# Gated network's first blocks: unpacking of down rows one block apart, earlier first rows, third unpacking pass of the last pieces on ScalarE

## The chip, the cores and the metric

The kernel runs on one core of a Trainium2 chip. The metric is device microseconds from start to end of one launch; 1810.05 is the median of three runs of the kernel before (1808.7 to 1810.61). The engines are TensorE (PE: matmuls), VectorE (DVE), ScalarE (ACT), GpSimd (POOL) and SyncE (SP: issues transfers). Each works through its own instruction list in order and waits only on semaphores.

## The reference, cut to what matters

Four layers run one after the other on x (8 x 256 rows of 512); this case lies in the first two.

```python
x = x + gamma * softmax_attention(layernorm(x), ctx, ctx)   # channels attend, 8 heads of 64
w_gu, w_down = fp4 codes * group scales                     # 4-bit values, packed 8 to a word
gate, up = layernorm(x) @ w_gu.T                            # 2 x 1408 columns
y = (silu(gate) * up) @ w_down.T
x = x + y / sqrt(mean(y * y) + eps)
x = x + quantised_attention(...)                            # not touched
x = x + ternary_ffn(...)                                    # not touched
```

## The kernel before, in words

**Mixing stage** (`mix_rows`, about 0 to 350 us). Sixteen tiles of 128 rows. In step j (j from -3 to 15, one per tile) TensorE makes the transposed scores of tile j (`tscore`, psT) and the row-major scores of tile j+1 (`score`, psS, three banks), weighs with `weigh` (psO, psE) behind slots 6 and 11 and at the end, and turns the row maxima (`turn_maxima`). A step has 16 slots n = 0 to 15, and on each engine the tables at the head of the function say in which slot a piece of work is issued. VectorE's main work is `greatest`: 16 row maxima of psS per tile, one bank each. A score into a bank waits until the maximum of the bank's former score is taken. Then `split` cuts the maxima into three parts, which TensorE turns, and `maxima_rows` makes of them what the next tile's scores subtract. ScalarE does the exponentials (`exp`), GpSimd the subtractions that make queries and keys (`queries`, `keys`), the first Newton steps (`roots`) and the end of a tile (`finish`).

**The packed weights.** The 512 x 2816 gate and up weights come as four row groups, each cut into four pieces of 704 columns: 16 pieces, k = 0 to 15. `unpack(k, i)` on VectorE takes a piece through three passes over 128 x 704: i = 0 shifts each word (`move_bits`), i = 1 masks it (`keep_bits`), i = 2 multiplies by 2^126 into f16 (w_gu). Piece k belongs to step k + 3; `BITS` names the slots of its three passes. Pieces 11 and 12 belong to step 14, pieces 13, 14 and 15 to step 15; of a step's pieces all but the first follow at the step's end, three passes each.

**First rows.** At the start of step 15 VectorE normalises the first 512 rows (`first_rows`). ScalarE rounds them to f16 in four quarters (`first_high`, slots `FIRST`), GpSimd makes the four remainders (first_lo), and two transposing transfers bring both to first_xT. The first gate product waits for both.

**Gated stage** (`gated_ffn`, about 350 to 700 us). Four columns t of 512 rows, in each 11 blocks p; m = 11 t + p counts them. A block is, on TensorE, 8 gate matmuls, half of the down matmuls that are due (`down`, from block m - 3), 8 up matmuls and the other half. Of the four row groups ScalarE scales two (`scale`, g_psG to g_sum), VectorE the other two (`fold`), GpSimd adds them (totalled). A block's groups go through four banks, so the up matmuls of a block wait for the gate's `scale` and `fold`. ScalarE's silu and VectorE's product (`hidden`, g_hT) of block m - 1 follow in block m. In the first column each block also unpacks a 128 x 512 piece of the down weights: `unpack_down` (VectorE, two passes, L799 and L804), `value_down` (ScalarE, L1025), `scale_down` (GpSimd, L876), all three for piece p in block p, so that ScalarE waits in block p for VectorE's passes of the same block before it comes to the scales of block p + 1. In blocks 5 to 8 follows a quarter of the next column: `normalise` (VectorE, L895), `high_part` (ScalarE, L998), `low_part` (GpSimd, L869).

Of the kernel before, what the change touches and what calls it, by code (L numbers as in the profile page):

```python
# [6 lines left out]
F32 = mybir.dt.float32  # L7
# [12 lines left out]
NT = TOK // P  # L20
# [20 lines left out]
SUBNORMAL = 2.0 ** -24  # L41
LOW_BYTES = 0x00FF00FF
LOG_SET = "natural_log_exp_and_others"


Programs = namedtuple("Programs", "sync gpsimd vector scalar tensor")
# [211 lines left out]
def mix_rows(env, x_in, ctx_in, ctxT_in, gu_in, gus_in):  # L258
# [13 lines left out]
    NT3 = 3  # L272
    NG = NU + 1
    WEIGH = (6, 11)
    FIRST = (10, 11, 12, 13)
    CUT_K, NORMAL, CUT_Q = (3, 5), (7, 8, 11, 12), (9, NU - 1)
    INVERT, STATS = (5, 8, 11, 14), (2, 13)
    UNPACK = {j: (j - 3,) for j in range(3, NT - 2)}
    UNPACK.update({NT - 2: (11, 12), NT - 1: (13, 14, 15)})
    BITS = (6, 10, 13)  # L280
    SCORES = [1 + (n in (1, 4, 7, 10)) if n < 12 else 0 for n in range(NU)]
    FIRST_SCORE = [sum(SCORES[:n]) for n in range(NU)]
    FETCH_GU = (2, 3, 8, 11)
# [2 lines left out]
    with ExitStack() as ctx:  # L286
# [6 lines left out]
        def sem(name):  # L293
# [47 lines left out]
        inverted, mixed_s, added, after_s, bits_s = (  # L341
            sem(f"m_{n}") for n in ("inverted", "mixed", "added", "after", "bits"))
        gu_loaded = [sem(f"m_gu_loaded{g}") for g in range(CH)]
        first_xn, first_hi, first_lo, scales_in = (
            sem(f"m_{n}") for n in ("first_xn", "first_hi", "first_lo", "scales_in"))
        xn, halves = xs[(NT - 3) % 3], (qs[(NT - 3) % 3], ks[(NT - 3) % 3])

        def rows4(src, j):
# [12 lines left out]
        def invert(v, j, h):  # L361

            if h == 0:
                v.wait_ge(o_read, 2 * (j + 1))
                if j:
                    v.wait_ge(mixed_s, j)
            at = slice(h * P, (h + 1) * P)
            v.reciprocal(rinv[:, at], e_sums[j % 2][:, at]).then_inc(inverted, 1)  # L368

        def after(v, j):  # L370

# [148 lines left out]
        def scalar(act):  # L520
            def roots(j):

                act.wait_ge(varied, HT * (j + 1))
                if j:
                    act.wait_ge(guessed, j)
                act.activation(lnv[:, :], mv[j % 2][:, :, 1], ACT.Ln, bias=eps[:, :]).then_inc(lnv_ready, 1)
                act.wait_ge(lnv_ready, j + 1)
                if j >= 2:
                    act.wait_ge(normed, j - 1)
                act.activation(guess[j % 2][:, :], lnv[:, :], ACT.Exp, scale=-0.5).then_inc(guessed, 1)  # L530

            def cut_keys(j, k):

                half = slice(2 * k, 2 * k + 2)
                if k == 0:
                    act.wait_ge(c_in_s[j % 2], 64 * (j // 2 + 1))
                if j:
                    act.wait_ge(k_ready, HT * (j - 1) + 2 * k + 2)
                act.activation(k_sub[:, half, :], cs[j % 2][:, half, :], ACT.Copy,
                               scale=k_lo[:, :]).then_inc(k_cut, 1)  # L540

            def normalise(j, h):

                if h == 0:
                    act.wait_ge(normed, j + 1)
                act.activation(xs[j % 3][:, h, :], xs[j % 3][:, h, :], ACT.Identity, scale=ys[j % 2][:, h:h + 1],
                               bias=away[j % 2][:, h:h + 1]).then_inc(normal, 1)

            def cut_queries(j, k):

                half = slice(2 * k, 2 * k + 2)
                act.wait_ge(normal, HT * j + 2 * k + 2)
                if j:
                    act.wait_ge(q_ready, HT * (j - 1) + 2 * k + 2)
                act.activation(q_sub[:, half, :], xs[j % 3][:, half, :], ACT.Copy,  # L555
                               scale=q_lo[:, :]).then_inc(q_cut, 1)

            def exp(j, n):
                g = NU * j + n
                act.wait_ge(tscored, g + 1)  # L560
                if g >= RING:
                    act.wait_ge(pv_done, g - RING + 1)
                act.activation(prob[:, g % RING, :], psT[g % NT3][:, :], ACT.Exp,  # L563
                               scale=float(D0) ** -0.5).then_inc(exped, 1)

            def collect(j):

                b = j % 2
                act.wait_ge(pv_done, NU * (j + 1))
                if j >= 2:  # L570
                    act.wait_ge(mixed_s, j - 1)
                    act.wait_ge(added, j - 1)
                act.activation(weighed[b][:, :], psO[:, :], ACT.Copy, scale=gamma[:, :]).then_inc(o_read, 1)
                act.activation(e_sums[b][:, :], psE[:, :], ACT.Copy).then_inc(o_read, 1)

            def first_high(k):

                if k == 0:
                    act.wait_ge(tscored, NU * (NT - 2))
                act.wait_ge(first_xn, k + 1)  # L580
                act.activation(halves[0][:, k, :], xn[:, k, :], ACT.Copy).then_inc(first_hi, 1)

            def steps(j):
                for n in range(NU):
                    if has(j):
                        exp(j, n)
                    if n == 0 and has(j - 1):
                        collect(j - 1)
                    if has(j + 2):
                        if n == 2:  # L590
                            roots(j + 2)
                        if n in CUT_K:
                            cut_keys(j + 2, CUT_K.index(n))
                        if n in NORMAL:
                            normalise(j + 2, NORMAL.index(n))
                        if n in CUT_Q:
                            cut_queries(j + 2, CUT_Q.index(n))
                    if j == NT - 1 and n in FIRST:
                        first_high(FIRST.index(n))
            nc.scalar.preload_act_table_set(LOG_SET)  # L600
            act.wait_ge(masks, 14)
            turns(steps)
            collect(NT - 1)

        def vector(v):
            def statistics(j, h):
# [45 lines left out]

            def unpack(k, i):

                g, at = k // PER, slice(k % PER * UW, (k % PER + 1) * UW)
                words = raw_gu[:, g % 2, at]
                if i == 0:
                    v.wait_ge(gu_loaded[g], 16)
                    move_bits(v, env, words).then_inc(bits_s, 1)
                if i == 1:  # L660
                    v.wait_ge(bits_s, 3 * k + 1)
                    keep_bits(v, words).then_inc(bits_s, 1)
                if i == 2:
                    v.wait_ge(bits_s, 3 * k + 2)
                    v.tensor_scalar(env["w_gu"][:, g, at], words.bitcast(F32), 2.0 ** 126, None,
                                    ALU.mult).then_inc(bits_s, 1)

            def first_rows():

# [137 lines left out]
def gated_ffn(env, dn_in, dns_in, last_tile):  # L807

    nc, x_sb, mv, rstd = (env[n] for n in ("nc", "x_sb", "mv", "rstd"))
    with ExitStack() as ctx:  # L810
# [53 lines left out]
        def gpsimd(pool):  # L864
# [13 lines left out]
            for t in range(NTC):  # L878
                for p in range(FG):
                    m = FG * t + p  # L880
                    for i in SIDES:
                        a, b = part_sum[0][i][m % 3], part_sum[1][i][m % 3]
                        pool.wait_ge(folded, 4 * m + 2 * i + 2)
                        pool.tensor_tensor(a[:, :], a[:, :], b[:, :], ALU.add).then_inc(totalled, 1)  # L884
                    if t == 0:
                        scale_down(p)
                    if p in SPLIT and t + 1 < NTC:
                        low_part(t + 1, SPLIT.index(p))

        def vector(v):  # L890
# [60 lines left out]
            for t in range(NTC):  # L951
                for p in range(FG):
# [10 lines left out]
                            take_y(t - 1, 2 * i + 1)  # L963
                    if m:
                        hidden(m - 1)
                    if t == 0:
                        unpack_down(p)
                        if p == 3:
                            aggregate(v, env, 0, NT)
                        if p == 4:  # L970
                            invert_roots(v, env, 0, NT)
# [20 lines left out]
        def scalar(act):  # L992
# [30 lines left out]
            def value_down(f):  # L1023
                act.wait_ge(dn_bits, 2 * f + 2)
                act.activation(w_dn[:, f, :], w_dn[:, f, :], ACT.Copy, scale=2.0 ** 126).then_inc(dn_valued, 1)  # L1025

            for t in range(NTC):
                for p in range(FG):
                    m = FG * t + p
                    if m >= 3:  # L1030
                        act.wait_ge(h_ready, m - 2)
                    for i in SIDES:
                        scale(m, i)
                        if t and p == TAKE:
                            square_y(t - 1, 2 * i)
                            square_y(t - 1, 2 * i + 1)
                    if m:
                        silu(m - 1)
                    if t == 0:
                        value_down(p)  # L1040
                    if p in SPLIT and t + 1 < NTC:
                        high_part(t + 1, SPLIT.index(p))
            silu(FG * NTC - 1)
# [3 lines left out]
        def tensor(pe):  # L1047
# [7 lines left out]

            def gate_up(t, p, i):
                at = (i * FG + p) * P
                for g in range(CH):
                    q = CH * (2 * (FG * t + p) + i) + g
                    free(q - CH)  # L1060
# [1064 lines left out]
```

## Time and profile before

| | |
|---|---|
| median of 3 runs | 1810.05 us |
| the profiled execution | 1810.41 us, span 1808.6 us |
| TensorE busy | 1703.9 us (94%) |
| VectorE busy | 1499.0 us (83%) |
| ScalarE busy | 1256.8 us (69%) |
| GpSimd busy | 907.0 us (50%) |
| 60 to 350 us (mixing) | TensorE 271.12, VectorE 278.37, ScalarE 232.53, GpSimd 185.43 busy of 290; granted clock 1.00 |
| 350 to 460 us (gated, first column) | TensorE 98.62, VectorE 79.13, ScalarE 53.64, GpSimd 59.31 busy of 110; granted clock 0.93 |
| 460 to 700 us | TensorE 239.06, VectorE 172.47 busy of 240; granted clock 1.00 |

The span is what the profiler saw between the first and the last instruction; about 1.8 us lie around it. A timeline row gives start, duration, engine, line, operation, output and inputs, shape and count; in brackets stands how long the engine was idle before it and who released it. Rows of one kind that follow each other are merged. A chain row is a piece of the path that ended last.

### The profile page before, as it was taken

Reading aid. Unit: us, or ns where it says so; the run is one execution under the profiler, and the core shown is the slowest. Engines: PE = TensorE matmul, PEld = TensorE weight load, DVE = VectorE, ACT = ScalarE, POOL = GpSimd, SP = SyncE. Lnnn points to the kernel's source line nnn. Section 1 sums busy time; section 2 is a strip of 40 time slices with the busy share of each in tenths; the row PEclk is TensorE's granted clock in tenths of the full one; section 3 lists DMA queues with packets and bytes.
Section 4 is the critical chain, followed back from the end, with each engine's and each line's share of the span. In section 5 each row is a group of like instructions: output and inputs, shape, how many; then the busy total and the mean of one; then the engine's idle time right before and its main releaser. Section 6 shows DMA issues by size and latency. Waiting matters only on the chain.

```text
span 1808.6 us, 30394 instructions
## 1 busy us (share of the span) xinstructions
PE 1703.9 (94%) x10706; PEld 744.6 (41%) x10706; DVE 1499.0 (83%) x2796; ACT 1256.8 (69%) x2111; POOL 907.0 (50%) x927
## 2 busy tenths in 40 slices
PE   4999999889999999989999999999999998999999
PEld 1332323234444444434444444444444444444444
DVE  6899999877767669787999999999999998883332
ACT  5888888455554442333799999999999996774433
POOL 6567666256445430000488888888888884000000
PEclk9999999989999999999999999999999999999999
DMA  9866651301011005556666666666666567112020
GB/s 222 222 149 134 156 137 42 117 3 24 1 24 44 20 1 168 100 105 124 115 111 107 107 110 105 114 112 113 117 112 109 105 110 240 24 24 47 24 47 24
DMA packets 420631, 170.45 MB, mean 94 GB/s; under 512 B 382080, under 2 KB 391296, under 8 KB 419328
## 3 DMA queue, kind: packets, MB, share of 16 engines
q1 hardware_dynamic: 420480, 168.51, 45.5%
q8 instruction: 85, 1.39, 0.3%
q14 instruction: 66, 0.54, 0.1%
HBM read 69.89 MB, written 4.19 MB: 41 GB/s over the span
## 4 chain that ended last, share of the span: by engine, by line
PE 67%; DVE 19%; ACT 5%; issue 5%; POOL 2%; DMA 1%; SPq 0%; DVEq 0%; ACTq 0%; POOLq 0%
PE a_psM L1541 12%; PE a_psS L1589 9%; PE g_psY L1075 7%; PE g_psG L1062 7%; PE t_psD L2052 6%; DVE rmax L627 5%; PE t_psU L2039 5%; PE a_psO L1601 4%; PE k_psA L1459 3%; PE psO L762 3%; PE psE L765 2%; DVE maxima L1555 2%; ACT a_prob L1677 2%; POOL a_wide L1657 2%; DVE rinv L368 1%
## 5 line engine op out<-in xcount | busy, mean ns | idle before, releaser
L1555 DVE TENSOR_REDUCE maxima<-a_psM 128x1 f32<-128x512 f32 x1024 | 623.4, 681 | 1.9 <-PE a_psM L1541 0.2
L1677 ACT ACTIVATE a_prob<-a_psS,maxima,q_scale 128x1024 uint8<-128x1024 f32 x512 | 610.8, 1210 | 17.0 <-PE a_psS L1589 14.7
L1657 POOL CAST a_wide<-a_pairs 128x2048 int16<-128x2048 uint8 x256 | 484.0, 1900 | 98.0 <-DMA a_pairs<-a_prob 89.9
L1541 PE MATMUL a_psM<-KT,QO 128*128 128x512 bf16 x1024 | 367.5, 383 | 5.2 <-DVE k_kn L1382 1.6
L1589 PE MATMUL a_psS<-KT,QO 128*128 128x512 bf16 x1024 | 305.7, 380 | 3.1 <-ACT a_prob L1677 3.1
L1601 PEld LDWEIGHTS a_psO<-V,a_wide 128*128 128x128 f16 x4096 | 175.2, 96 | 140.5 <-DVE QO L1630 23.0
L1601 PE MATMUL a_psO<-V,a_wide 128*128 128x32 bf16 x4096 | 181.3, 177 | 16.4 <-DVE QO L1630 15.6
L905 DVE SCALAR_TENSOR_TENSOR g_sum<-g_psG,gu_scale,g_sum 128x512 f32<-128x512 f32 x176 | 124.1, 745 | 86.4 <-PE g_psG L1062 71.2
L884 POOL TENSOR_TENSOR g_sum<-g_sum 128x512 f32<-128x512 f32 x88 | 125.8, 1430 | 128.7 <-DVE g_sum L905 128.7
L563 ACT ACTIVATE prob<-psT 128x512 f32<-128x512 f32 x256 | 143.1, 599 | 60.7 <-PE psT L750 60.2
L1010 ACT ACTIVATE g_sum<-g_psG,gu_scale 128x512 f32<-128x512 f32 x176 | 111.5, 682 | 103.8 <-PE g_psG L1062 102.9
L627 DVE TENSOR_REDUCE rmax<-psS 128x1 f32<-128x512 f32 x256 | 158.6, 675 | 11.9 <-PE psS L736 9.7
L1075 PE MATMUL g_psY<-raw_dn,g_hT 128*128 128x512 f32 x352 | 163.1, 592 | 0.0
L1541 PEld LDWEIGHTS a_psM<-KT,QO 128*128 128x128 bf16 x1024 | 97.1, 96 | 132.2 <-DVE maxima L1555 127.2
L1864 DVE TENSOR_TENSOR t_hT_lo<-t_h,t_hT_hi 128x512 f16<-128x512 f32 x64 | 44.3, 692 | 123.4 <-ACT t_hT_hi L1991 123.3
L736 PE MATMUL psS<-ks,qs 128*128 128x512 f16 x256 | 91.1, 388 | 36.0 <-POOL qs L488 20.7
L1589 PEld LDWEIGHTS a_psS<-KT,QO 128*128 128x128 bf16 x1024 | 97.5, 98 | 66.7 <-ACT a_prob L1677 8.6
L1644 POOL TENSOR_TENSOR maxima<-maxima,q_scale 128x2 f32<-128x2 f32 x128 | 25.2, 197 | 190.0 <-DVE maxima L1549 190.0
L488 POOL TENSOR_TENSOR qs<-xs,q_sub 128x512 f16<-128x512 f32 x64 | 76.0, 1209 | 79.5 <-ACT q_sub L555 78.9
L1980 ACT ACTIVATE t_h<-t_psU,t_b 128x512 f32<-128x512 f32 x64 | 43.7, 682 | 92.6 <-PE t_psU L2039 92.6
L1677 ACT ACTIVATION_READ_ACCUMULATOR a_prob<-a_psS,maxima,q_scale 128x1 f32 x512 | 103.9, 203 | 0.0
L2052 PE MATMUL t_psD<-QO,t_hT_hi 128*128 128x512 f16 x256 | 97.1, 379 | 4.6 <-DVE x_sb L1875 3.4
(219 smaller groups left out, 2755.1 us busy)
## 6 DMA issues: line engine op xcount, KB each, us to landing
xs<-in_x SPq DMA_DIRECT2D x64, 256.0 KB, 6.9
cs<-in_ctx SPq DMA_DIRECT2D x64, 256.0 KB, 8.9
KT<-in_w SPq DMA_DIRECT2D x2, 4096.0 KB, 19.1
raw_gu<-in_gu SPq DMA_DIRECT2D x4, 1408.0 KB, 8.6
vs<-in_ctxT SPq DMA_DIRECT2D x16, 256.0 KB, 3.0
a_pairs<-a_prob SPq DMA_TRANSPOSE x256, 3.0
out<-x_sb SPq DMA_DIRECT2D x16, 256.0 KB, 2.6
x_sb<-in_x SPq DMA_DIRECT2D x1, 3584.0 KB, 14.4
```

Source lines behind the costliest of these rows:

```text
L563: act.activation(prob[:, g % RING, :], psT[g % NT3][:, :], ACT.Exp, scale=float(D0) ** -0.5).then_inc(exped, 1)
L627: v.reduce_max(rmax[j % 2][:, n:n + 1], psS[(NG * j + n) % 3][:, :], AX.X).then_inc(maxed, 1)
L884: pool.tensor_tensor(a[:, :], a[:, :], b[:, :], ALU.add).then_inc(totalled, 1)
L1062: mm = pe.matmul(psG[q % CH][:, :], w_gu[:, g, at:at + P], xT[t % 2][s][:, :, g, :], start=(s == 0), stop=(s == 1))
L1075: mm = pe.matmul(psY[k][:, :], hT[t % 2][:, f, k * P:(k + 1) * P], w_dn[:, f, :], start=(f == 0), stop=(f == FG - 1))
L1541: pe.matmul(psM[n % NM][:, :], QOf[:, i * P:(i + 1) * P], KTf[:, keys:keys + 512], start=True, stop=True).then_inc(shown, 1)
L1555: v.reduce_max(tops[i // JOIN % NB][:, i % JOIN, c:c + 1], psM[n % NM][:, :], AX.X).then_inc(topped, 1)
L1589: mm = pe.matmul(psS[g % NS][:, c * 512:(c + 1) * 512], QOf[:, i * P:(i + 1) * P], KTf[:, keys + c * 512:keys + (c + 1) * 512], start=True ...
L1601: mm = pe.matmul(psO[:, h * D1:(h + 1) * D1], wide[i % NV][:, parity, c, :].bitcast(F16), V[:, 2 * c + parity, h, :], start=(parity == 0 a ...
L1657: pool.tensor_copy(wide[i % NV][:, :, :, :].rearrange("p k c q -> p k (c q)"), both).then_inc(widened, 1)
L1677: act.activation(prob[i % NP][:, k * HK:(k + 1) * HK], psS[g % NS][:, :], ACT.Exp, scale=q_scale[:, i:i + 1], bias=bias[i // JOIN % NB][:, ...
L2052: mm = pe.matmul(psD[k][:, :], hT[s][:, g % RING, k * P:(k + 1) * P], w2q(f), start=(f == 0 and s == 0), stop=(f == FC - 1 and s == 1))
```

## The change

The diff has four parts.

1. `BITS` goes from (6, 10, 13) to (2, 6, 10). It holds for every step that unpacks, 3 to 15. `UNPACK` moves piece 12 from step 14's end to step 15.
2. `FIRST` goes from slots 10 to 13 to slots 7 to 10.
3. The third pass of pieces 12 to 15 moves from VectorE to ScalarE (`value_gu`): piece 12 in slot 12 of step 15, the others behind the last `collect`. The first gate product and the first up product wait for it. ScalarE loads the silu table ahead of the gated stage.
4. In the gated stage VectorE unpacks down piece m - 1 in block m (1 to 11), and ScalarE and GpSimd take piece m - 2 in block m (2 to 12).

```diff
-    FIRST = (10, 11, 12, 13)
+    FIRST = (7, 8, 9, 10)
+    LAST_GU = 12
...
-    UNPACK.update({NT - 2: (11, 12), NT - 1: (13, 14, 15)})
-    BITS = (6, 10, 13)
+    UNPACK.update({NT - 2: (11,), NT - 1: (12, 13, 14, 15)})
+    BITS = (2, 6, 10)
...
+            def value_gu(k):
+
+                act.wait_ge(bits_s, bits_of(k) + 2)
+                act.activation(gu_place(k), gu_words(k).bitcast(F32), ACT.Copy, scale=2.0 ** 126).then_inc(gu_valued, 1)
...
+                    if j == NT - 1 and n == 12:
+                        value_gu(LAST_GU)
...
             collect(NT - 1)
+            for k in range(LAST_GU + 1, CH * PER):
+                value_gu(k)
...
-                if i == 2:
+                if i == 2 and k < LAST_GU:
```

In the gated stage, on GpSimd, VectorE, ScalarE and TensorE in this order:

```diff
-                    if t == 0:
-                        scale_down(p)
+                    if 2 <= m < FG + 2:
+                        scale_down(m - 2)
...
+                    if 1 <= m <= FG:
+                        unpack_down(m - 1)
                     if t == 0:
-                        unpack_down(p)
...
+            nc.scalar.preload_act_table_set(SILU_SET)
...
-                    if t == 0:
-                        value_down(p)
+                    if 2 <= m < FG + 2:
+                        value_down(m - 2)
...
+                if t == 0 and p == 0:
+                    pe.wait_ge(env["gu_valued"], 1 + 3 * i)
```

VectorE's order in a mixing step, from the first maxima of a tile on (rmax: `greatest`; raw_gu with shift: first pass; raw_gu: second; w_gu: third). Before:

```order
L627 TENSOR_REDUCE rmax<-psS 128x1 x4
L613 BN_STATS stats<-xs 128x6
L627 TENSOR_REDUCE rmax<-psS 128x1 x4
L368 RECIPROCAL rinv<-e_sums 128x128
L627 TENSOR_REDUCE rmax<-psS 128x1
L799 TENSOR_SCALAR raw_gu<-raw_gu,shift 128x704
L627 TENSOR_REDUCE rmax<-psS 128x1 x3
L368 RECIPROCAL rinv<-e_sums 128x128
L627 TENSOR_REDUCE rmax<-psS 128x1 x3
L804 TENSOR_SCALAR raw_gu<-raw_gu 128x704
L627 TENSOR_REDUCE rmax<-psS 128x1
```

and after the change:

```order
L651 TENSOR_REDUCE rmax<-psS 128x1 x4
L637 BN_STATS stats<-xs 128x6
L821 TENSOR_SCALAR raw_gu<-raw_gu,shift 128x704
L651 TENSOR_REDUCE rmax<-psS 128x1 x4
L371 RECIPROCAL rinv<-e_sums 128x128
L651 TENSOR_REDUCE rmax<-psS 128x1
L826 TENSOR_SCALAR raw_gu<-raw_gu 128x704
L651 TENSOR_REDUCE rmax<-psS 128x1 x3
L371 RECIPROCAL rinv<-e_sums 128x128
L651 TENSOR_REDUCE rmax<-psS 128x1 x3
L688 TENSOR_SCALAR w_gu<-raw_gu 128x704
L651 TENSOR_REDUCE rmax<-psS 128x1
```

The first pass now stands ahead of the fifth maximum instead of behind the ninth, the second where the first stood, the third where the second stood; the place of the third, behind the split of the maxima, is empty.

ScalarE's order from the last exponentials of the mixing stage into the first gated blocks (qs<-xs: `first_high`; w_gu: `value_gu`; raw_dn: `value_down`). Before:

```order
L563 ACTIVATE prob<-psT 128x512 x2
L573 ACTIVATE weighed<-psO,gamma 128x512
L574 ACTIVATE e_sums<-psE 128x512
L1010 ACTIVATE g_sum<-g_psG,gu_scale 128x512 x4
L1025 ACTIVATE raw_dn<-raw_dn 128x512
L1010 ACTIVATE g_sum<-g_psG,gu_scale 128x512 x4
L1003 ACT_TABLE_LOAD
L1003 ACTIVATE g_sum<-g_sum 128x512
L1025 ACTIVATE raw_dn<-raw_dn 128x512
L1010 ACTIVATE g_sum<-g_psG,gu_scale 128x512 x4
```

and after the change:

```order
L601 ACTIVATE w_gu<-raw_gu 128x704
L578 ACTIVATE prob<-psT 128x512 x3
L588 ACTIVATE weighed<-psO,gamma 128x512
L589 ACTIVATE e_sums<-psE 128x512
L601 ACTIVATE w_gu<-raw_gu 128x704 x3
L1050 ACT_TABLE_LOAD
L1033 ACTIVATE g_sum<-g_psG,gu_scale 128x512 x8
L1026 ACTIVATE g_sum<-g_sum 128x512
L1033 ACTIVATE g_sum<-g_psG,gu_scale 128x512 x4
L1026 ACTIVATE g_sum<-g_sum 128x512
L1048 ACTIVATE raw_dn<-raw_dn 128x512
L1033 ACTIVATE g_sum<-g_psG,gu_scale 128x512 x4
```

The two exponentials at the head of the first excerpt are the last ones of the tile. In the second, ScalarE takes the piece of slot 12 and the three behind the tile's end, then loads the table; the scales of blocks 0 and 1 then follow each other with nothing of the down weights between them.

## Rows read from the trace of the kernel before

**Rows 1.** Chain of waits, 198 to 240 us: start, us, what (excerpt)
```profile
216.75 0.60 DVE rmax L627
...
217.48 0.38 PE psS L736
```

**Rows 2.** Timeline, VectorE, one tile: start, us, line, operation, count, [idle<-releaser]
```profile
213.66 2.48 DVE L627 TENSOR_REDUCE rmax<-psS 128x1 f32<-128x512 f32 x4
...
220.45 0.57 DVE L799 TENSOR_SCALAR raw_gu<-raw_gu,shift 128x704 int32<-128x704 int32 x1
221.15 1.89 DVE L627 TENSOR_REDUCE rmax<-psS 128x1 f32<-128x512 f32 x3
...
225.55 1.08 DVE L804 TENSOR_SCALAR raw_gu<-raw_gu 128x704 int32<-128x704 int32 x1
...
228.59 0.18 DVE L641 TENSOR_TENSOR rparts<-rrest,rparts 128x16 bf16<-128x16 f32 x1
...
229.28 0.51 DVE L665 TENSOR_SCALAR w_gu<-raw_gu 128x704 f16<-128x704 f32 x1
...
233.49 2.48 DVE L627 TENSOR_REDUCE rmax<-psS 128x1 f32<-128x512 f32 x4
```

**Rows 3.** Timeline, VectorE, tiles with no packed pieces
```profile
75.11 2.48 DVE L627 TENSOR_REDUCE rmax<-psS 128x1 f32<-128x512 f32 x4 [1.62 <-PE psS L736]
...
82.60 1.89 DVE L627 TENSOR_REDUCE rmax<-psS 128x1 f32<-128x512 f32 x3 [0.62 <-PE psS L736]
...
94.70 2.48 DVE L627 TENSOR_REDUCE rmax<-psS 128x1 f32<-128x512 f32 x4 [0.96 <-PE psS L736]
```

**Rows 4.** Timeline, TensorE, the tile of Rows 2
```profile
228.82 0.24 PE L774 MATMUL psS<-id_b,rparts 128*51 128x128 bf16 x1 [0.17 <-DVE rparts L641]
```

**Rows 5.** Timeline, GpSimd, the tile of Rows 2
```profile
218.30 4.85 POOL L477 TENSOR_TENSOR ks<-cs,k_sub 128x512 f16<-128x512 f32 x4
225.09 2.56 POOL L488 TENSOR_TENSOR qs<-xs,q_sub 128x512 f16<-128x512 f32 x2 [1.94 <-ACT q_sub L555]
```

**Rows 6.** Timeline, ScalarE, last tile and first gated blocks
```profile
337.26 2.06 ACT L563 ACTIVATE prob<-psT 128x512 f32<-128x512 f32 x4 [1.62 <-PE psT L750]
339.19 0.65 ACT L581 ACTIVATE qs<-xs 128x512 f16<-128x512 f32 x1
...
365.24 1.28 ACT L1003 ACT_TABLE_LOAD   x1
```

**Rows 7.** Timeline, GpSimd, last tile and first gated blocks
```profile
339.98 5.51 POOL L515 TENSOR_TENSOR ks<-xs,qs 128x512 f16<-128x512 f32 x4 [9.46 <-ACT qs L581]
...
362.40 2.49 POOL L884 TENSOR_TENSOR g_sum<-g_sum 128x512 f32<-128x512 f32 x2
```

**Rows 8.** Timeline, TensorE, first gate product
```profile
350.61 0.59 PE L1062 MATMUL g_psG<-first_xT_hi,w_gu 128*128 128x512 f16 x1 [4.09 <-DMA first_xT_lo<-ks]
```

**Rows 9.** Waits, 330 to 430 us: who waited for whom, us, times, longest
```profile
ACT raw_dn L1025 <- DVE raw_dn L804: 31.8, 9, 4.9
...
PE g_psG L1062 <- ACT g_sum L1010: 10.0, 6, 4.0
```

**Rows 10.** Timeline, VectorE, gated blocks
```profile
371.14 1.41 DVE L905 SCALAR_TENSOR_TENSOR g_sum<-g_psG,gu_scale,g_sum 128x512 f32<-128x512 f32 x2 [1.27 <-ACT g_sum L1010]
...
407.08 0.68 DVE L915 TENSOR_TENSOR g_hT<-g_sum 128x512 f32<-128x512 f32 x1
407.68 1.49 DVE L799 TENSOR_SCALAR raw_dn<-raw_dn,shift 128x512 int32<-128x512 int32 x1
409.21 0.43 DVE L804 TENSOR_SCALAR raw_dn<-raw_dn 128x512 int32<-128x512 int32 x1
...
414.50 0.68 DVE L915 TENSOR_TENSOR g_hT<-g_sum 128x512 f32<-128x512 f32 x1
```

**Rows 11.** Timeline, GpSimd, gated blocks
```profile
407.25 1.65 POOL L884 TENSOR_TENSOR g_sum<-g_sum 128x512 f32<-128x512 f32 x1 [0.47 <-DVE g_sum L905]
410.38 1.16 POOL L876 TENSOR_TENSOR raw_dn<-raw_dn,dn_scale 128x512 f32<-128x512 f32 x1 [1.49 <-ACT raw_dn L1025]
```

More of the change, by code:

```diff
@@ L43 @@
 LOG_SET = "natural_log_exp_and_others"
+SILU_SET = "silu_and_others"
 Programs = namedtuple("Programs", "sync gpsimd vector scalar tensor")
@@ L343, in mix_rows @@
         gu_loaded = [sem(f"m_gu_loaded{g}") for g in range(CH)]
-        first_xn, first_hi, first_lo, scales_in = (
-            sem(f"m_{n}") for n in ("first_xn", "first_hi", "first_lo", "scales_in"))
+        first_xn, first_hi, first_lo, scales_in, gu_valued = (
+            sem(f"m_{n}") for n in ("first_xn", "first_hi", "first_lo", "scales_in", "gu_valued"))
+        env["gu_valued"] = gu_valued
         xn, halves = xs[(NT - 3) % 3], (qs[(NT - 3) % 3], ks[(NT - 3) % 3])
@@ L368, in invert, with gu_words, gu_place, bits_of @@
             v.reciprocal(rinv[:, at], e_sums[j % 2][:, at]).then_inc(inverted, 1)
+        def gu_words(k):
+            return raw_gu[:, k // PER % 2, k % PER * UW:(k % PER + 1) * UW]
+        def gu_place(k):
+            return env["w_gu"][:, k // PER, k % PER * UW:(k % PER + 1) * UW]
+        def bits_of(k):
+            return 3 * min(k, LAST_GU) + 2 * max(0, k - LAST_GU)
         def after(v, j):
@@ L653, in unpack @@
             def unpack(k, i):
-                g, at = k // PER, slice(k % PER * UW, (k % PER + 1) * UW)
-                words = raw_gu[:, g % 2, at]
+                words = gu_words(k)
                 if i == 0:
-                    v.wait_ge(gu_loaded[g], 16)
+                    v.wait_ge(gu_loaded[k // PER], 16)
                     move_bits(v, env, words).then_inc(bits_s, 1)
                 if i == 1:
-                    v.wait_ge(bits_s, 3 * k + 1)
+                    v.wait_ge(bits_s, bits_of(k) + 1)
                     keep_bits(v, words).then_inc(bits_s, 1)
-                if i == 2:
-                    v.wait_ge(bits_s, 3 * k + 2)
-                    v.tensor_scalar(env["w_gu"][:, g, at], words.bitcast(F32), 2.0 ** 126, None,
-                                    ALU.mult).then_inc(bits_s, 1)
+                if i == 2 and k < LAST_GU:
+                    v.wait_ge(bits_s, bits_of(k) + 2)
+                    v.tensor_scalar(gu_place(k), words.bitcast(F32), 2.0 ** 126, None, ALU.mult).then_inc(bits_s, 1)
             def first_rows():
```

## The prediction

> **What bounds the kernel now.** I read the chain of waits first, then each engine's timeline around its stations. In the mixing stage the path changes between VectorE and TensorE. In a tile in the middle, the fifth row maximum ends a stretch of VectorE and releases TensorE's score [rows 1]: TensorE's score stands at 217.48, right behind the maximum's end at 217.35. The path then lies on TensorE (scores, weighing), and comes back to VectorE at 221.15, where the tenth maximum waits for a score: the first unpacking pass ended at 220.45 + 0.57 = 221.02, so it lay in time in which VectorE would have waited anyway [rows 2]. In a tile without packed pieces that gap is visible, 0.62 us idle at 82.60 [rows 3]. The last maxima, with the second pass between them, are on VectorE's path, and TensorE waits 0.17 us at the turn of the maxima [rows 4]. The third pass stands behind that, where TensorE weighs and nobody waits. So three passes (0.57 + 1.08 + 0.51 us [rows 2]) cost only 0.24 us of a tile: it takes 233.49 - 213.66 = 19.83 us [rows 2] against 94.70 - 75.11 = 19.59 without them [rows 3]. Their places decide.
>
> In the gated stage's first column ScalarE waits 31.8 us for VectorE's passes over the down words, and TensorE 10.0 us for ScalarE's scales behind them [rows 9]. That wait goes with the change. The question is who is late next.
>
> **How long a pass takes.** The pass of 1.08 us starts at 225.55, while a GpSimd instruction pair runs from 225.09 [rows 5]; a single one of that pair ends about 1.14 later (half of the pair, less what VectorE holds), at 226.23, and the pass ends at 226.63, 0.4 behind that [rows 2]. The pass at 220.45 meets the change from the second to the third of four GpSimd instructions that began at 218.30 [rows 5], near 220.58, and pays 0.57. The one at 229.28 meets none and pays 0.51. I take it that a pass costs 0.43 from start to the next start, plus the rest of the GpSimd instruction that it meets. The Trainium skill says so too (SBUF — State Buffer, Who interferes with whom): VectorE's two-port modes and GpSimd share a port pair, and the one that starts later is blocked for the other's whole instruction, while a tensor_reduce never is. The durations above agree. By that rule passes that meet GpSimd's work can't be counted at their own length, which speaks against two parts of this change.
>
> **BITS earlier, steps 3 to 12 (ten tiles).** The first pass now stands ahead of the fifth maximum, on the path. It meets only GpSimd's short steps there: 0.43 to 0.6, I take 0.5. TensorE's score and weighing are later by that. The second pass follows where the first stood, at 220.45 + 0.5 = 220.95, in the third of the four instructions, which (with the first pass gone from there) ends at 218.30 + 3 x 1.14 = 221.72. So it ends at about 222.15, where the tenth maximum stood at 221.15: it is now 1.0 later, of which TensorE's lateness hides 0.5. The third pass replaces the second. Queries' first instruction is 0.5 later too (225.6, ends 226.74), so the third pass, ready at 225.55 + 1.0, ends near 227.2 where the second ended at 226.63: VectorE is 0.6 late at the turn. TensorE, 1.0 late since the waited score, used to wait 0.17 there and is 0.83 late. The later of the two counts: 0.84 a tile, 8.4 us for ten. The empty place behind the split gives nothing back: TensorE weighs there. Bounds: if the second pass meets no instruction, 0.43 - 0.17 = 0.26 a tile, 2.6 us; if each pass meets a whole further one, 1.3 a tile, 13 us. In steps 13 and 14 there are fewer statistics ahead of the fifth maximum, and in 14 no queries and keys: from the same terms 0.6 + 0.2 = 0.8 us (0 to 1.5). Together 9.2 us later.
>
> **Piece 12 and FIRST.** VectorE has the first rows some 2.8 us sooner, but ScalarE's first quarter stands right behind an exponential that TensorE paces: at 339.19, behind four from 337.26 [rows 6]. Three exponentials of 0.48 now come behind it: 1.4 us. GpSimd's four remainders (339.98, 5.51 us [rows 7]) still alternate with VectorE's passes, now of pieces 13 to 15, so they start and end 1.4 sooner, and with them the first gate product at 350.61, which waits for the second transfer [rows 8]. It gains 1.4 us.
>
> **Third pass on ScalarE.** A 512-wide activation there takes 0.5 from start to start [rows 6], so 704 columns take about 0.7. One in slot 12 lies in waits for TensorE. Three behind the tile's end, 2.1 us, fall into the transfer's time, and so does a part of the table load, 1.28 us, which today stands ahead of the first silu [rows 6]. What sticks out delays the first fold, by my estimate by 0.4 us of those 1.28. The Trainium skill (ScalarE: Activation LUTs, What ACT_TABLE_LOAD costs) adds a drain of 1.38 us to each load; in this trace the next activation starts at once behind the load, and with the drain the sum below would be 1.4 us higher.
>
> **Down words one block apart.** TensorE and ScalarE no longer wait for the passes, so blocks 0 and 1 run into each other. Next late is GpSimd. It ends the last tile's `finish` behind VectorE's reciprocals, and then adds (two at 362.40, 2.49 us [rows 7]). With the net 1.4 - 0.4 = 1.0 us from above it starts them at 361.4 and ends at 363.9. The product of block 0 meets the next addition (363.9 + 1.25 + 0.6 = 365.75), the first pass another one (365.75 + 1.25 + 0.4 = 367.4), the second takes 0.4: the folds of block 2 start at 367.8 instead of 371.14 [rows 10], 3.4 us sooner. From there on VectorE's own chain is the bound, with each block as long as before: GpSimd's scaling no longer waits for ScalarE, so it follows its additions at once, and the second pass meets it. In block 5, where TensorE has its down products too, a little more can come: I take 3.8 us of gain by its end.
>
> In blocks 5 to 8 the path is product, first pass, second pass, next rows' quarter, ScalarE's high half, scales, TensorE, folds: 414.50 - 407.08 = 7.42 us [rows 10]. There the addition at 407.25 (1.65 [rows 11]) makes the first pass 1.49 long, and the second takes 0.43, because GpSimd's scaling starts only at 410.38, 1.49 us after the addition [rows 11]. One block apart its input lies ready: it starts when the first pass ends, at 409.2, holds 1.16 us, and the second pass ends at 410.8 instead of 409.6. ScalarE's waiting, which the change removes, gives only 0.1 here, since the high half waits for VectorE's quarter behind the pass. So 4 x 1.15 = 4.6 us are lost. Later blocks are TensorE's. The gated stage: -3.8 + 4.6 = +0.8 us (-8 to +6).
>
> **Sum.** 1810.4 (span 1808.6 + 1.8 around it) + 9.2 + 0.8 = 1820.4. The profiled execution is 0.4 above the median, so 1820.0 us.
>
> **Rivals.**
> - *Light passes* (0.20): the second pass in slot 6 finds GpSimd's port free and GpSimd's early scaling doesn't win it from the second down pass. Mixing 10 x 0.43 + 0.5 = 4.8, less the gated gain of 3.8: +1.0, 1811.1. If only the first half of this holds, 4.8 + 0.8 = 5.6: 1815.7 (0.06 of the 0.20). For it: the pass at 220.45 was lucky already. Against it: most of the 1.08 us passes were not.
> - *ScalarE's wait was the price* (0.08), the faster side: TensorE gets back most of its 10.0 us [rows 9], say 8, at the gated stage's start, and the mixing stage takes only its lower bound of 2.6. It decides as soon as VectorE is through with block m's passes before block m + 1's first bank is needed: 1804.6. Against it: the sum of product and passes behind two additions.
> - *Heavier passes* (0.15): 1.3 a tile: 13 + 1.5 + 0.8 = 15.3, 1825.4. For it: every pass that is delayed reaches further into the next GpSimd instruction. Against it: the first pass meets only short ones.
> - *My forecast* has 0.57, with its own range 1816 to 1823.
>
> About 0.2%, 3.6 us, is what a measurement tells from no change here. Slower by more: the forecast, the heavier passes and 0.06 of the light ones, 0.78. Within: the other 0.14 of the light. Faster: 0.08. The range that leaves out 2 in 10 goes from 1811 to 1825.
>
> **What the profile would show.** Right: steps 3 to 12 take 20.5 to 20.8 us each instead of 19.83; TensorE's idle time ahead of the eighth score grows by 0.5; the second pass in slot 6 takes about 1.1 us; the first gate product stands 1.4 us closer to the last weighing's start; in blocks 5 to 8 L826 (the second pass) takes 1.5 us and a block 8.5. Wrong: tiles of 19.8 to 20.1 us, or second down passes of 0.43 us.

## The result, and the profile after

The change costs 0.8%: 1823.92 us, median of 4 runs (1823.17 to 1824.1), against 1810.01 of the kernel before beside them (1808.7 to 1810.61). The ratio is 1.0083, 95% interval 1.0072 to 1.0095. The forecast was 1820.0, +10.0; it is +13.9.

Page of the changed kernel, engines' busy time:

```profile
span 1821.4 us, 30395 instructions
...
PE 1705.0 (94%) x10706; PEld 742.1 (41%) x10706; DVE 1511.9 (83%) x2792; ACT 1259.2 (69%) x2115; POOL 908.0 (50%) x927
```

TensorE has the same work (1703.9 us before), VectorE is busy 12.9 us more. I cut both spans at the same instructions:

| stretch | before | after | difference | forecast |
|---|---|---|---|---|
| up to step 3 | 94.70 | 94.50 | -0.2 | 0 |
| steps 3 to 12, ten tiles | 198.27 | 209.85 | +11.6 | +8.4 |
| step 13 | 19.31 | 19.99 | +0.7 | +0.6 |
| step 14 to the first gate product | 38.33 | 36.65 | -1.7 | -1.2 |
| from there to block 5's product (g_hT) | 49.06 | 44.87 | -4.2 | -2.4 |
| four blocks, 5 to 9 | 29.66 | 32.73 | +3.1 | +4.6 |
| four blocks, 9 to 13 | 27.57 | 31.54 | +4.0 | 0 |
| the rest, by difference | 1351.7 | 1351.3 | -0.5 | 0 |

The differences are taken before rounding. The sum is +12.8, the difference of the spans (1821.4 - 1808.6).

**Mixing stage.** Timeline of the changed kernel, VectorE, two neighbouring tiles; it answers [rows 2]:

```profile
199.87 2.48 DVE L651 TENSOR_REDUCE rmax<-psS 128x1 f32<-128x512 f32 x4 [0.54 <-PE psS L758]
...
207.16 1.24 DVE L826 TENSOR_SCALAR raw_gu<-raw_gu 128x704 int32<-128x704 int32 x1
...
212.71 0.62 DVE L688 TENSOR_SCALAR w_gu<-raw_gu 128x704 f16<-128x704 f32 x1
...
220.41 2.48 DVE L651 TENSOR_REDUCE rmax<-psS 128x1 f32<-128x512 f32 x4 [0.76 <-PE psS L758]
...
223.41 0.57 DVE L821 TENSOR_SCALAR raw_gu<-raw_gu,shift 128x704 int32<-128x704 int32 x1
...
227.69 1.52 DVE L826 TENSOR_SCALAR raw_gu<-raw_gu 128x704 int32<-128x704 int32 x1
...
233.52 1.46 DVE L688 TENSOR_SCALAR w_gu<-raw_gu 128x704 f16<-128x704 f32 x1
...
241.84 2.48 DVE L651 TENSOR_REDUCE rmax<-psS 128x1 f32<-128x512 f32 x4 [0.54 <-PE psS L758]
```

Tiles alternate between 220.41 - 199.87 = 20.54 us and 241.84 - 220.41 = 21.43 us; the mean is 20.985, 1.16 over 19.83. The first pass takes 0.57 in both, as forecast. The second and third decide the length: 1.24 and 0.62 in the short tile, 1.52 and 1.46 in the long one. GpSimd and TensorE in the long tile:

```profile
225.43 4.79 POOL L492 TENSOR_TENSOR ks<-cs,k_sub 128x512 f16<-128x512 f32 x4
232.32 2.28 POOL L503 TENSOR_TENSOR qs<-xs,q_sub 128x512 f16<-128x512 f32 x2 [2.10 <-ACT q_sub L570]
```

```profile
224.72 0.38 PE L758 MATMUL psS<-ks,qs 128*128 128x512 f16 x1 [0.88 <-DVE rmax L651]
...
229.96 0.38 PE L758 MATMUL psS<-ks,qs 128*128 128x512 f16 x1 [0.31 <-DVE rmax L651]
```

The queries' second instruction would start at 232.32 + 1.14 = 233.46, just where VectorE's third pass does (233.52): the pass meets the whole of it. The second pass meets the third key instruction in the same way (225.43 + 2 x 1.14 = 227.71, pass at 227.69). Ahead of the fifth maximum TensorE waits 0.88 us, where it was 0.38 before, and 0.31 behind the second pass. The long tile is 0.89 us longer than the short one, and its third pass takes 0.84 more; GpSimd starts its keys 225.43 - 220.41 = 5.02 us behind the first maxima there, in the short tile 4.75. Why the tiles alternate was not tested.

**Last tile.** Timelines of the changed kernel, ScalarE and then TensorE; they answer [rows 6, 8]:

```profile
350.30 0.62 ACT L596 ACTIVATE qs<-xs 128x512 f16<-128x512 f32 x1
...
354.99 0.78 ACT L601 ACTIVATE w_gu<-raw_gu 128x704 f16<-128x704 f32 x1
...
360.54 2.14 ACT L601 ACTIVATE w_gu<-raw_gu 128x704 f16<-128x704 f32 x3
362.70 1.28 ACT L1050 ACT_TABLE_LOAD   x1
363.99 1.27 ACT L1033 ACTIVATE g_sum<-g_psG,gu_scale 128x512 f32<-128x512 f32 x2
```

```profile
360.99 0.38 PE L1088 MATMUL g_psG<-first_xT_hi,w_gu 128*128 128x512 f16 x1 [1.66 <-issue]
```

Three third passes take 2.14 us, as worked out, and the next activation stands right behind the table load: the drain that the Trainium skill adds (ScalarE: Activation LUTs, What ACT_TABLE_LOAD costs) doesn't show here either. The first gate products follow a wait of 1.66 us where it was 4.09 [rows 8], and run at full clock. Windows (us, busy time and instructions of each engine, granted clock PEclk, DMA share, GB/s), first the kernel before, then the changed one:

```profile
350.00:356.00 6.00, 5.39 (x14) 2.01 (x15) 2.46 (x4) 2.26 (x4) 0.00 (x0) 0.54 0.86 331
```

```profile
360.00:366.00 6.00, 3.06 (x14) 1.15 (x14) 1.29 (x2) 5.78 (x9) 0.00 (x0) 1.00 1.01 326
```

0.54 is near the lower level, 1.2 GHz, 1.00 the upper, 2.4 GHz. It isn't what the stretch to block 5 gains by, as e3 and e4 show below.

**Gated stage.** VectorE in the changed kernel, first blocks and one block of 5 to 8, and GpSimd in the latter; they answer [rows 10, 11]:

```profile
376.00 1.67 DVE L937 TENSOR_TENSOR g_hT<-g_sum 128x512 f32<-128x512 f32 x1 [2.57 <-POOL g_sum L906]
377.59 1.48 DVE L821 TENSOR_SCALAR raw_dn<-raw_dn,shift 128x512 int32<-128x512 int32 x1
...
379.45 1.40 DVE L927 SCALAR_TENSOR_TENSOR g_sum<-g_psG,gu_scale,g_sum 128x512 f32<-128x512 f32 x2
...
414.04 0.68 DVE L937 TENSOR_TENSOR g_hT<-g_sum 128x512 f32<-128x512 f32 x1
414.64 1.49 DVE L821 TENSOR_SCALAR raw_dn<-raw_dn,shift 128x512 int32<-128x512 int32 x1
416.17 1.26 DVE L826 TENSOR_SCALAR raw_dn<-raw_dn 128x512 int32<-128x512 int32 x1
...
422.22 0.68 DVE L937 TENSOR_TENSOR g_hT<-g_sum 128x512 f32<-128x512 f32 x1
```

```profile
414.21 1.64 POOL L906 TENSOR_TENSOR g_sum<-g_sum 128x512 f32<-128x512 f32 x1 [0.47 <-DVE g_sum L927]
415.81 1.33 POOL L898 TENSOR_TENSOR raw_dn<-raw_dn,dn_scale 128x512 f32<-128x512 f32 x1
```

GpSimd's scaling now follows its addition at once and lies under the second pass: 1.26 us instead of 0.43, and a block of 422.22 - 414.04 = 8.18 us instead of 7.42. In these blocks TensorE waits for the scaling too, ahead of its down product. First TensorE's row, then ScalarE's, its four scales of the block:

```profile
417.29 1.96 PE L1101 MATMUL g_psY<-raw_dn,g_hT 128*128 128x512 f32 x4 [0.80 <-POOL raw_dn L898]
```

```profile
418.45 2.63 ACT L1033 ACTIVATE g_sum<-g_psG,gu_scale 128x512 f32<-128x512 f32 x4
```

The scales start 422.22 - 418.45 = 3.77 us ahead of the next product, as before the change (414.50 - 410.73). So the path over the longer second pass is as tight as it was, and the path over TensorE's wait ends beside it, within about 0.1 us: by these rows, taking either away alone would not bring 7.42 back. By the wait's path alone a block would take about the 7.9 us of blocks 9 to 12 (an estimate); e6 below has a block with the longer pass and no such wait, 8.25 us.

In blocks 9 to 12 the scaling stands on the path. Chain of waits of the changed kernel (start, us, what), and TensorE there:

```profile
437.93 0.75 DVE g_sum L927
...
438.75 1.65 POOL g_sum L906
440.40 1.31 POOL raw_dn L898
...
441.84 1.96 PE g_psY L1101 x4
443.80 1.31 PE g_psG L1088 x6
```

```profile
441.84 1.96 PE L1101 MATMUL g_psY<-raw_dn,g_hT 128*128 128x512 f32 x4 [0.81 <-POOL raw_dn L898]
```

The down products of block m need the scaled piece m - 3. With the scaling of piece m - 2 in block m, they are due hardly a block later, and the loop addition, scaling, down product, next product, fold closes: 31.54 / 4 = 7.89 us a block instead of 6.89.

### The profile page after: what moved, and what is told of

Its sections match the earlier page's. It is cut to its first block, busy times and chain, and to the rows that moved or that the text cites. A ratio compares the mean times of both kernels' runs of the same rounds, so it can differ in the third digit from the quotient of the medians.

```text
span 1821.4 us, 30395 instructions
## 1 busy us (share of the span) xinstructions
PE 1705.0 (94%) x10706; PEld 742.1 (41%) x10706; DVE 1511.9 (83%) x2792; ACT 1259.2 (69%) x2115; POOL 908.0 (50%) x927
## 4 chain that ended last, share of the span: by engine, by line
DVE 45%; PE 45%; issue 4%; ACT 3%; POOL 2%; DMA 0%; SPq 0%; DVEq 0%; ACTq 0%; POOLq 0%
DVE maxima L1581 26%; PE g_psY L1101 7%; PE g_psG L1088 6%; DVE rmax L651 6%; PE t_psD L2078 6%; PE t_psU L2065 5%; PE k_psA L1485 3%; PE a_psM L1567 3%; PE psO L784 2%; PE psE L787 2%; PE a_psS L1615 2%; DVE rinv L371 2%; PE k_psA L1467 1%; PE a_psO L1627 1%; PE psT L768 1%
```

## The experiments

They ran in three groups, each beside its own runs of the kernel before: 1811.09 (1806.98 to 1818.05) for the first four, 1810.12 (1806.55 to 1811.62) for the next four, 1808.8 (1807.08 to 1811.85) for the last.

**e1_bits_only: the early slots alone.** The kernel before with

```diff
-    BITS = (6, 10, 13)
+    BITS = (2, 6, 10)
```

> The kernel before, with BITS (2, 6, 10) alone. Theory (slots): the first pass ahead of the fifth maximum and the second pass behind two GpSimd instructions cost 11.6 us in steps 3 to 12 and 0.7 in step 13, whatever else the change does: +12 us, 1822, tiles alternating between 20.5 and 21.4 us. Rival (the rest takes part): the longer steps need the rest of the change, or the empty place behind the split gives something back: +4 to +8, 1814 to 1818.

Measured: 1820.42 (1818.86 to 1822.42), ratio 1.0054 [1.0035, 1.0074]. Tiles 21.44 and 20.54 us in turn, ten of them 209.90, and step 13 19.99: the changed kernel's numbers to 0.05. The mixing stage's loss in these eleven steps is the slots' and nothing else's. The medians differ by 9.3 us only, less than the tiles' 12.3; the kernel before's own runs in this group reach up to 1818.05 (see e4).

**e2_bits_back: the change without the early slots.** The changed kernel with

```diff
-    BITS = (2, 6, 10)
+    BITS, LAST_BITS = (6, 10, 13), (2, 6, 10)
...
+                    bits = LAST_BITS if j == NT - 1 else BITS
```

> The changed kernel, with slots (6, 10, 13) again in steps 3 to 14 and (2, 6, 10) in step 15 only. Theory (slots): tiles of 19.83 us again, 1823.9 - 12.3 = 1811.6, which leaves +1.6 for the three other parts. Rival: the three other parts are a gain or a loss of their own of over 5 us, 1805 or 1816.

Measured: 1811.68 (1809.92 to 1812.71), ratio 1.0002 [0.999, 1.0014]. Tiles of 19.82 are back. The stretches of the table above: 36.13 us from step 14 to the first gate product, 44.76 on to block 5's product, then 32.73 and 31.55. So everything but the slots sums to about nothing: -2.2 - 4.3 + 3.1 + 4.0 = +0.6.

**e3_no_down_shift: e2 with the down words as before** (piece p in block p on VectorE, ScalarE and GpSimd).

```diff
-                    if 2 <= m < FG + 2:
-                        scale_down(m - 2)
+                    if t == 0:
+                        scale_down(p)
```

(and so for `unpack_down` and `value_down`)

> The kernel of e2 with the down words unpacked, converted and scaled as before (all three in block p). Left of the change: earlier first rows, piece 12 in step 15, third pass of the last pieces on ScalarE, early table load. Theory: the first gate product comes 1.5 us earlier against step 14's start and the table load of 1.28 us leaves the wait for the first silu: -2 to -3 us, 1807.5. Rival: block 0's wait for the down words' passes swallows it, since GpSimd's finish ends no earlier: 1810.

Measured: 1810.33 (1805.31 to 1817.99), ratio 0.9998 [0.998, 1.0015]. 36.15 to the first gate product, 2.2 less than before: first rows, ScalarE's third passes and the early table load bring that together; no run takes them apart. Then 48.84 (-0.2), 29.66 and 27.57 as before. The -2.4 don't show in the median: its runs spread over 12.7 us, and in its profile three of ten tiles take 20.94 us, which adds 3.3. More on such tiles stands under e4.

**e4_down_shift_only: the kernel before with the down words one block apart,** and no more.

```diff
-                    if t == 0:
-                        scale_down(p)
+                    if 2 <= m < FG + 2:
+                        scale_down(m - 2)
```

(and so for `unpack_down` and `value_down`)

> The kernel before, with the down words one block apart alone. Theory (early scaling): about 2.5 to 4 us gained up to block 5, 3.1 lost in blocks 5 to 8 (second pass 1.26 us instead of 0.43), 4.0 lost in blocks 9 to 12 (TensorE waits for GpSimd's scaling): +3 to +4, 1813.5. Rival: the loss is of the first rows' or ScalarE's parts, and the shift gives back the waits of TensorE for ScalarE, up to 10 us: 1802 to 1806.

Measured: 1814.08 (1812.55 to 1820.74), ratio 1.0026 [1.0012, 1.0041]. 44.20 to block 5 (-4.9), 32.72 (+3.1), 31.54 (+4.0): +2.2 net, so the shift by itself loses. The clock doesn't make the 4.9: its first products take 0.58 to 0.63 us, as those of the kernel before do. The granted clock of the whole stretch is 0.91 here and 0.85 before, and e3, with 0.90, gains 0.2. Its mixing stage is the kernel before's code, and yet seven of its ten profiled tiles take 20.94 us instead of 19.83. One of them, VectorE and GpSimd:

```profile
177.12 2.48 DVE L627 TENSOR_REDUCE rmax<-psS 128x1 f32<-128x512 f32 x4
...
183.90 1.50 DVE L799 TENSOR_SCALAR raw_gu<-raw_gu,shift 128x704 int32<-128x704 int32 x1
...
189.72 1.48 DVE L804 TENSOR_SCALAR raw_gu<-raw_gu 128x704 int32<-128x704 int32 x1
```

```profile
181.63 4.79 POOL L477 TENSOR_TENSOR ks<-cs,k_sub 128x512 f16<-128x512 f32 x4
```

Keys start 4.51 us behind the first maxima here, 4.64 in [rows 2, 5]. The third key instruction (181.63 + 2 x 1.14 = 183.91) comes as the pass does, and the pass takes 1.50 instead of 0.57. The 4.51 are the long form's own, though: in the first long tile (from 114.29) the keys start 4.60 us behind the first maxima and the pass takes 1.58.

**e5_first_pass_only: the first pass early, slot 6 empty, the others as before.** The kernel before with

```diff
-    BITS = (6, 10, 13)
+    BITS = (2, 10, 13)
```

> The kernel before, with BITS (2, 10, 13): only the first pass moved, to the place ahead of the fifth maximum; slot 6 is left empty. Theory (two prices: the place on VectorE's path, and the instructions of GpSimd that a pass meets in slot 6): the place alone costs 0.4 to 0.5 us a tile, so tiles of 20.2 to 20.4 us that all have one length, +4.5 against the kernel before at its fastest (1807), 1811.5. Rival (the place is all): tiles of 20.98 on average as with all three moved, 1819 to 1820.

Measured: 1815.57 (1812.31 to 1817.69), ratio 1.003 [1.0018, 1.0041]. All tiles 20.34 us. VectorE, one tile:

```profile
199.37 0.58 DVE L799 TENSOR_SCALAR raw_gu<-raw_gu,shift 128x704 int32<-128x704 int32 x1
...
204.37 1.89 DVE L627 TENSOR_REDUCE rmax<-psS 128x1 f32<-128x512 f32 x3 [0.62 <-PE psS L736]
...
208.76 1.09 DVE L804 TENSOR_SCALAR raw_gu<-raw_gu 128x704 int32<-128x704 int32 x1
```

The first pass costs its full start-to-start time, 0.51 a tile (20.34 - 19.83), and where it used to lie there is the idle 0.62 of [rows 3]. The remaining 20.985 - 20.34 = 0.64 is the other two passes' new places; no run moves one of them alone.

**e9_slots_behind_split: all three passes where TensorE weighs.** The kernel before with

```diff
-    BITS = (6, 10, 13)
+    BITS = (12, 13, 14)
```

> The kernel before, with BITS (12, 13, 14): all three passes behind the split of the maxima, where GpSimd stands idle and TensorE weighs. Theory (port): the kernel before has tiles of 19.83 and of 20.94 us, by whether its first pass in slot 6 comes to the port 0.1 us ahead of GpSimd's third key instruction or behind it; with no pass there all tiles take 19.6 to 19.7 and its runs lie within 2 us of each other at 1805. Rival: the passes delay what VectorE does there for the next tile, the first maximum comes later, tiles of 20.3 to 20.7: 1813 to 1816.

Measured: 1808.86 (1806.3 to 1811.36), ratio 0.9996 [0.9987, 1.0005]. VectorE, from the end of one tile into the next:

```profile
207.76 0.58 DVE L799 TENSOR_SCALAR raw_gu<-raw_gu,shift 128x704 int32<-128x704 int32 x1
...
208.86 0.51 DVE L804 TENSOR_SCALAR raw_gu<-raw_gu 128x704 int32<-128x704 int32 x1
...
210.15 0.47 DVE L665 TENSOR_SCALAR w_gu<-raw_gu 128x704 f16<-128x704 f32 x1
...
213.02 0.38 DVE L619 BATCH_NORM_AGGREGATE mv<-stats 128x2 f32<-128x6 f32 x4
213.31 2.45 DVE L627 TENSOR_REDUCE rmax<-psS 128x1 f32<-128x512 f32 x4
```

No pass meets GpSimd, and still the tile is 19.82, not the shorter one I expected: VectorE reaches its next maxima without a gap, so the room behind the split is used up: [rows 3] show 0.96 us of idle time there, less than the three passes need. All ten tiles have one length, but the runs spread over 5 us, more than expected. Step 13 is 0.3 shorter.

**e8_no_scaling: e2 without GpSimd's scaling of the down words.** Left out is the multiplication by dn_scale; TensorE waits for ScalarE's conversion instead.

```diff
-                    if 2 <= m < FG + 2:
-                        scale_down(m - 2)
...
-                        pe.wait_ge(dn_ready, f + 1)
+                        pe.wait_ge(dn_valued, f + 1)
```

> The kernel of e2 without GpSimd's scaling of the down words (that multiplication is left out; TensorE waits for ScalarE's conversion instead). Theory (port): the second down pass takes 0.43 us again instead of 1.26, blocks 5 to 8 take 7.3 to 7.4 us instead of 8.18, blocks 9 to 12 6.9 instead of 7.93: 7 us less than e2, 1804.5. Rival (VectorE's chain is long by itself, or TensorE waits for ScalarE's conversion next): blocks 5 to 8 stay above 8, or 9 to 12 above 7.5.

Measured: 1802.64 (1801.24 to 1803.85), ratio 0.9959 [0.9944, 0.9974]. VectorE, one block of 5 to 8, and TensorE's down product in blocks 9 to 12:

```profile
407.26 0.68 DVE L936 TENSOR_TENSOR g_hT<-g_sum 128x512 f32<-128x512 f32 x1
407.86 1.49 DVE L822 TENSOR_SCALAR raw_dn<-raw_dn,shift 128x512 int32<-128x512 int32 x1
409.38 0.43 DVE L827 TENSOR_SCALAR raw_dn<-raw_dn 128x512 int32<-128x512 int32 x1
```

```profile
427.69 1.88 PE L1100 MATMUL g_psY<-raw_dn,g_hT 128*128 128x512 f32 x4
```

The second pass is 0.43 again, four blocks are 29.40 and 27.55, and TensorE no longer waits ahead of its down product. Both late losses (3.3 and 4.0 us against e2) hang on the scaling, and another 1.5 us up to block 5 (43.23), which I had not expected. The run takes away GpSimd's work and TensorE's wait together; that the second pass pays by meeting the instruction and TensorE by waiting for its result is read from the rows, not told apart by this run. Without the multiplication it prices the scaling and is no kernel to use.

**e6_shift_then_same: the shift only where it gains.** e2, with the pieces converted and scaled one block behind VectorE in blocks 1 to 4, and in the same block again from 5 on.

```diff
+        SAME = 5
+        def DOWN_OF(m):
+            if m < SAME:
+                return [m - 1] if m else []
+            return [SAME - 1, SAME] if m == SAME else [m] if m < FG else []
...
-                    if 2 <= m < FG + 2:
-                        scale_down(m - 2)
+                    for f in DOWN_OF(m):
+                        scale_down(f)
...
+                    if m == 1:
+                        unpack_down(0)
...
-                    if 1 <= m <= FG:
-                        unpack_down(m - 1)
+                    if 1 <= m < FG:
+                        unpack_down(m)
```

(and so for `value_down`)

> The kernel of e2 with another schedule of the down words: in blocks 1 to 4 ScalarE and GpSimd take the piece of the block before, from block 5 on that of the same block, as before the change; VectorE unpacks piece 0 ahead of the first product, while it waits for GpSimd, and from then on piece p in block p. Theory: it keeps the gain of the first blocks (4 us between the first gate product and the end of block 5, less up to 1 for the extra piece in block 5), and has 7.41 us in blocks 5 to 8 and 6.89 in 9 to 12: 5 to 7 us less than e2, 1805.5. Rival: VectorE's two passes ahead of the first product wait for GpSimd's instructions and delay the product, the gain of the first blocks goes: 1809.

Measured: 1806.52 (1805.01 to 1808.19), ratio 0.9985 [0.9976, 0.9993]. 36.12 and 46.24 to block 5, then 30.50 (one block of 8.25, three of 7.42) and 27.57. VectorE, the block from 394.52 and the one from 402.77:

```profile
394.52 0.68 DVE L945 TENSOR_TENSOR g_hT<-g_sum 128x512 f32<-128x512 f32 x1
...
396.65 1.26 DVE L827 TENSOR_SCALAR raw_dn<-raw_dn 128x512 int32<-128x512 int32 x1
...
402.77 0.68 DVE L945 TENSOR_TENSOR g_hT<-g_sum 128x512 f32<-128x512 f32 x1
...
404.90 0.43 DVE L827 TENSOR_SCALAR raw_dn<-raw_dn 128x512 int32<-128x512 int32 x1
```

In the first of them the scaling of piece 4 still meets the second pass, and the block takes 8.25 us although TensorE never waits for the scaling in this run: 7.42 + 0.83 of the longer pass is all of it, though ScalarE and GpSimd take a second piece in this block too. From the next block on, with ScalarE's conversion behind VectorE again, GpSimd comes late enough to miss the second pass. It keeps -2.2 - 2.8 + 0.8 = -4.2 us of the sum.

**e7_shift_and_slots: e6 and e9 together.** e6 with

```diff
-    BITS, LAST_BITS = (6, 10, 13), (2, 6, 10)
+    BITS, LAST_BITS = (12, 13, 14), (2, 6, 10)
```

> The kernel of e6 with slots (12, 13, 14) in steps 3 to 14, all passes behind the split of the maxima. Theory: the two add up. Ten tiles of 19.82 us, none of 20.94, the two after them 0.9 us shorter together, and the gated stage of e6: 0 to 1 us less than e6, ratio to the kernel before 0.998, 1806. Rival: step 14's passes behind the split delay the first rows, which stand next on VectorE, and with them the first gate product: over 1 us more than e6.

Measured: 1805.9 (1804.55 to 1806.87), ratio 0.9982 [0.9973, 0.9991]. 36.13, 46.22, 30.50, 27.57, and step 13 at 19.01: -4.5 by the segments. That is 0.2% less than the kernel before, with an interval clear of 1, as for e6. Its ratio and e6's overlap, so the slots add nothing that can be told.

## Why the prediction was right or wrong, point by point

- **The first pass, on the path, about 0.5 a tile: right.** It took 0.57, and e5 prices its place at 0.51.
- **Slots 6 and 10, 0.84 a tile in all: the first step that failed.** The working describes the short tile: it has a second pass of 1.20 us (1.24 measured), a third of about 0.65 (0.62) and 0.84 a tile (0.71). It took that tile for all ten. Every other tile is the long one: the second pass meets the third key instruction from that one's start (1.52), and the third pass meets the queries' second instruction and not the end of their first (1.46). The mean is 1.16 a tile, 11.6 us for ten where 8.4 stood. The rival of heavier passes had 1.3. The light rival counts 0.43 a tile where the working's own bound for the same case has 0.26, 1.7 us too much for ten; nothing hangs on it.
- **First rows, 1.4 sooner: short by half a microsecond.** The first quarter did stand right behind an exponential (350.30, behind 349.80). The stretch gained 1.7 where 1.2 stood (1.4 less step 14's 0.2), and e3 has 2.2 for the same edits with the old slots ahead of them.
- **Block 2's folds 3.4 us sooner: right.** They start at 379.45 - 324.34 = 55.11 behind step 14's start; before, 371.14 - 312.28 = 58.86: 3.75 sooner. GpSimd's additions and the two passes behind them came as the working had them.
- **"From there on ... each block as long as before": failed.** TensorE's lateness in those blocks (VectorE waits 1.15 us for it ahead of one fold before) was ScalarE's waiting too, and it went: 5.9 us are gained by block 5 where 3.6 stood (3.8 less step 14's 0.2). e4 shows the shift's own share, 4.9.
- **Blocks 5 to 8, 1.15 each: mechanism right, 0.77 measured.** The scaling starts at 415.81, 0.36 before the second pass, so less of it is left (pass 1.26, not 1.59). e8 confirms that the scaling is the cause, and e6's block of 8.25 that the longer pass is enough. TensorE's wait of 0.80 for the scaling in the same blocks was not in the working.
- **"Later blocks are TensorE's": the step that failed outright.** I looked only at VectorE's side of the moved scaling. Its consumer is the down product three blocks on from the piece's own, and one block apart twice (VectorE, then ScalarE and GpSimd) leaves it no room. +4.0 us. Reading who waits for L876's result, and in which block, would have shown it.

The two failures add 3.2 (mixing) and 4.0 (late blocks); the larger gain by block 5 (-2.3, the first rows within it) and the cheaper second pass (-1.5) take off 3.8. With step 13 and the two ends (-0.6) the spans come 2.8 above the forecast; the medians, measured in other runs, 3.9. The rival of ScalarE's wait is refuted for its sign, not its effect: 4 to 5 us of the wait do come back (e2 against e3, e4), but the same edit loses 7 later.

## What to carry to other kernels

Before an operation is issued a block earlier, ask where it lands on every engine: whose passes it will now meet, and when its consumer needs it. Here a delay of one block helped at the stage's start, where the engines wait for each other, and harmed in the steady part, where the old wait kept two engines apart and the consumer had no room; it could be had for the first blocks alone (e6). An empty place on an engine is worth what its neighbours wait for there: passes that cost 0.24 us of a tile in waiting time cost 1.4 three and four slots earlier.

## What the runs showed of the hardware

**One code, two tile lengths.** The mixing code of the kernel before ran in tiles of 19.83 and of 20.94 us. Its own profile has only the short ones; the long ones stand in the profiles of e4 (seven of ten), whose mixing code is the same, and e3 (three of ten). By the rows, less than 0.05 us between VectorE's first pass and GpSimd's third key instruction tips a tile: the first long tiles have their keys 4.59 and 4.60 us behind the first maxima, short ones of the same profiles 4.60 to 4.62. The long form then puts the keys at 4.51 and so keeps itself up, and both profiles leave it in the same step, 11, where the keys wait 0.14 us for TensorE and start at 4.69 and 4.70. It fits the spread of the kernel before over 1807 to 1818 us in one group of runs, and it can let an edit at one place move time at another. That it makes that spread was not shown: in the other two groups the kernel before stays within 5.1 us, and e2, with the same slots in steps 3 to 12 and in the same group as e3 and e4, stays within 2.8.

**GpSimd's instruction and VectorE's pass, back to back.** A pass takes 0.43 (512 wide) to 0.58 us alone and up to 1.6 when it comes as a GpSimd instruction of 1.14 starts. The Trainium skill's rule (SBUF — State Buffer, Who interferes with whom) says that the later one waits for the other's whole instruction. The rows agree, in both directions: where the pass comes first, in the short tiles of the kernel before, the third key instruction lies 1.46 us ahead of the fourth, where 1.12 us lie between the others. A maximum, a reduction, took 0.62 to 0.69 in every run.
